# Odd query tiles' attention probabilities transposed by a trip through DRAM and VectorE instead of TensorE

## The reference

```
Q = x @ Wq;  K = ctx @ Wk;  V = ctx @ Wv            (8 heads)
score = Q K^T / sqrt(512), masked;  attn = softmax(score over the 77 keys)
out = concat_heads(attn @ V) @ Wo + x
y = (out - mean(out)) * rsqrt(var(out) + 1e-5) * gamma + beta
```

## Time and profile before

| | |
|---|---|
| time, three runs | 354.24 us median (353.8 to 354.63) |
| span of the profiled execution | 352.2 us |
| time around the span (median less span) | 2.0 us |
| PE busy | 346.3 us, 98% |
| DVE / ACT / POOL busy | 81% / 69% / 61% |
| TensorE's granted clock | full speed throughout |
| DMA | 55.81 MB, mean 158 GB/s |

### The profile page before, as it was taken

The page is one execution under the profiler, slowest core; times in us unless marked ns, Lnnn a source line. Parts: engine busy times, 40 slices in busy tenths (PEclk is TensorE's granted clock), DMA queues, the critical chain, the costliest instruction groups (busy, mean ns, idle before and its releaser), DMA issues.

```text
span 352.2 us, 6867 instructions
## 1 busy us (share of the span) xinstructions
PE 346.3 (98%) x2272; PEld 322.7 (92%) x2272; DVE 285.9 (81%) x523; ACT 243.3 (69%) x796; POOL 213.2 (61%) x218
## 2 busy tenths in 40 slices
PE   8999999999999999999999999999999999999994
PEld 6999999999999999998899899889988998999884
DVE  0159999999778767898798888987987989889896
ACT  3267766545777679887886976977778769768460
POOL 0045654400447958689769678688696696884243
PEclk9999999999999999999999999999999999999999
DMA  7998669775644080043152341440532413413012
GB/s 234 428 416 334 265 222 337 288 259 211 220 152 198 0 292 11 1 179 125 57 179 64 118 151 60 152 147 36 180 105 75 162 71 129 149 47 105 32 50 100
DMA packets 19683, 55.81 MB, mean 158 GB/s; under 512 B 1728, under 2 KB 3264, under 8 KB 17728
## 3 DMA queue, kind: packets, MB, share of 16 engines
q1 hardware_dynamic: 18784, 54.38, 42.8%
q10 hardware_dynamic: 864, 1.00, 1.0%
HBM read 46.98 MB, written 8.39 MB: 157 GB/s over the span
## 4 chain that ended last, share of the span: by engine, by line
PE 97%; DMA 1%; DVE 0%; DVEq 0%; issue 0%
PE pair L681 30%; PE pair L606 27%; PE pair L489 20%; PE pair L496 13%; PE pair L668 5%; PE pair L596 1%; PE pair L698 1%; DMA w_proj<-wk 1%; DVE centred L1199 0%; DVEq L105 0%; DVE stats_last L1191 0%; DVE mean_var L1196 0%; DVE var_eps L1171 0%; PE pair L616 0%; DVE out_sb L1185 0%
## 5 line engine op out<-in xcount | busy, mean ns | idle before, releaser
L1373 POOL TENSOR_TENSOR w_proj_lo<-w_proj,w_proj_hi 128x768 fp32r<-128x768 f32 x20 | 36.6, 1850 | 73.0 <-ACT w_proj_hi L766 73.0
L681 PE MATMUL pair<-vw_hi,pt_hi 128*128 128x512 f32 x155 | 62.3, 402 | 0.0
L681 PE MATMUL pair<-vw_hi,pt_lo 128*128 128x512 f32 x155 | 60.8, 392 | 0.0
L681 PE MATMUL pair<-vw_lo,pt_hi 128*128 128x512 f32 x155 | 60.6, 391 | 0.0
L1322 POOL TENSOR_TENSOR out_sb<-centred,beta_sb 128x512 f32<-128x512 f32 x30 | 38.9, 1296 | 28.9 <-ACT centred L875 28.8
L830 ACT ACTIVATE prob<-c,neg_max 128x77 f32<-128x77 f32 x128 | 44.0, 346 | 0.0
L489 PE MATMUL pair<-kv_t,w_out_hi 128*128 128x308 f32 x160 | 41.7, 334 | 0.0
L1367 POOL TENSOR_TENSOR xo_lo<-x_sum,xo_hi 128x512 fp32r<-128x512 f32 x32 | 41.4, 1299 | 0.2 <-ACT xo_hi L854 0.2
L606 PE MATMUL pair<-a_hi,xo_hi 128*128 128x308 f32 x128 | 40.4, 315 | 0.0
L606 PE MATMUL pair<-a_hi,xo_lo 128*128 128x308 f32 x128 | 38.9, 304 | 0.0
L606 PE MATMUL pair<-a_lo,xo_hi 128*128 128x308 f32 x128 | 38.9, 304 | 0.0
(11 more groups left out here) (117 smaller groups left out, 1015.1 us busy)
## 6 DMA issues: line engine op xcount, KB each, us to landing
w_out<-wo SPq DMA_DIRECT2D x8, 1024.0 KB, 4.8
xt_in<-x_tiles SPq DMA_DIRECT2D x16, 512.0 KB, 4.1
x_in<-x_rows SPq DMA_DIRECT2D x16, 512.0 KB, 4.9
out<-out_sb SPq DMA_DIRECT2D x31, 256.0 KB, 2.2
w_out<-wq_t SPq DMA_DIRECT2D x7, 1024.0 KB, 8.0
w_proj<-wv SPq DMA_DIRECT2D x8, 768.0 KB, 4.9
w_proj<-wk SPq DMA_DIRECT2D x6, 768.0 KB, 9.7
w_out<-wq_t SPq DMA_DIRECT2D x2, 512.0 KB, 8.0
```

What stands on the lines that cost most here:

```text
L681: mm = pe.matmul(ps_out[:, i % 2, 0:s.model], ps[:, j, :], v[:, j, b, :], start=(j == 0 and n == 0), stop=(j == s.key_t - 1 and n == len(p ...
L1373: pool.tensor_tensor(half_cols(w_proj_lo[u % W_RING], half), half_cols(w_proj_sb[u % W_RING], half), half_cols(w_proj_hi[u % 2], half).bit ...
```

## The change

Tiles 3, 5, ... 29 (fourteen, one in each iteration p = 2 to 15) no longer pass through PE's transposes. For them SP waits for the normalised probabilities, writes them to a DRAM tensor "shelf" in two DMAs (shelve), waits for these to land, and reads them back in four DMAs (take_back) into an SBUF tile "turned" in which the four 32-row groups of the queries and the four 32-key groups have changed places. DVE then turns 32x32 blocks in two instructions (turn) into ps_pt, after which ACT and DVE split as before. The even tiles, and tiles 1 and 31, stay on PE. DVE runs turn(a-1) where it ran split_pt(a-1), and split_pt(a-1) after normalise(a); ACT runs split_pt(a-1) after exps_first(p) instead of before it. The blocks need a key order with a stride: a group of 128 keys is now every third key of the first 384, or every second of the last 256 (key_tile), in prob and in VW alike, and both are padded from 616 to 640 keys with zeros. So VW's groups 0 to 2 are turned in uses 13, 14, 15 and groups 3 and 4 both in stage 2's first_products(0), where before they went in uses 10, 12, 13, 15 and one in first_products(0).

```diff
 def transposes_during(s):
-    plan, j = [], 0
-    for h in range(s.heads + 1):
-        ready = []
-        while j < s.key_t and j * P + s.key_rows(j) <= s.keys * h:
...
+    plan = [[] for _ in range(s.heads + 1)]
+    (_, first), _ = s.parts()
+    for j in range(first):
+        plan[s.heads - first + j] = [(j, b) for b in range(s.batches)]
+    plan[s.heads] = [(j, b) for b in range(s.batches) for j in range(first, s.key_t)]
...
+        turned = sb("turned", [P, P // QUAD, s.key_t * QUAD])
+        shelf = [nc.dram_tensor(f"shelf{n}", [P, P // QUAD, s.key_t * QUAD], F32, kind="Internal")
+                 for n in range(2)]
...
+        def key_tile(t, j):
+            first, count = s.parts()[j >= s.parts()[1][0]]
+            return t[:, first * P + j - first:(first + count) * P:count]
+        def by_dma(i):
+            return i % 2 == 1 and 3 <= i < LAST
...
+            def shelve(i):
+                n = dma_before(i)
+                sp.wait_ge(dve_prob, i + 1)
+                for first, count in s.parts():
+                    sp.dma_start(shelf[n % 2][:, :, first * QUAD:(first + count) * QUAD],
+                                 prob[i % 2][:, first * P:(first + count) * P].rearrange("p (c n) -> p c n", c=P // QUAD))\
+                      .then_inc(shelved[n % 2], DMA_INC)
+            def take_back(i):
+                n = dma_before(i)
+                sp.wait_ge(shelved[n % 2], 2 * use(n, 2))
+                if n > 0:
+                    sp.wait_ge(dve_turned, 2 * n)
+                by_quad = shelf[n % 2].rearrange("(r q) c n -> c q r n", q=QUAD)
+                for c in range(P // QUAD):
+                    sp.dma_start(turned[c * QUAD:(c + 1) * QUAD, :, :], by_quad[c]).then_inc(back, DMA_INC)
...
                 t = i - OUT_RING
+                if t >= 0 and by_dma(i):
+                    shelve(i)
+                    take_back(i)
...
                 for j in range(s.key_t):
-                    rows = s.key_rows(j)
-                    mm = pe.transpose(ps_pt[0:rows, j // 4, (j % 4) * P:(j % 4 + 1) * P],
-                                      prob[i % 2][:, j * P:j * P + rows], identity[:, :])
+                    mm = pe.transpose(ps_pt[:, j // 4, (j % 4) * P:(j % 4 + 1) * P],
+                                      key_tile(prob[i % 2][:, :], j), identity[:, :])
...
                 out_rows(a - 3)
-                transpose_prob(a - 1)
                 product_s3(p)
...
             def split_pt(i):
-                act.wait_ge(pe_pt, i + 1)
+                if by_dma(i):
+                    act.wait_ge(dve_turned, 2 * dma_before(i + 1))
+                else:
+                    act.wait_ge(pe_pt, pe_before(i + 1))
...
+                exps_first(p)
                 split_pt(a - 1)
-                exps_first(p)
                 scale(a - 3)
...
+            def turn(i):
+                dve.wait_ge(back, DMA_INC * (P // QUAD) * dma_before(i + 1))
+                dve.wait_ge(dve_pt_lo, i)
+                for first, count in s.parts():
+                    blocks = pt_blocks[:, first:first + count, :].rearrange("p j (r q) -> p r j q", q=QUAD)
+                    rows = turned[:, :, first * QUAD:(first + count) * QUAD].rearrange("p r (q j) -> p r j q", j=count)
+                    dve.transpose(blocks, rows).then_inc(dve_turned, 1)
...
-            split_vw(H, [0])
+            split_vw(plan[H][:1])
             add_w2(0)
             max_c11(0)
+            split_vw(plan[H][1:2])
             combine_c22(0)
             combine_c12(0)
             combine_c21(0)
-            split_vw(H, [1])
+            split_vw(plan[H][2:])
             normalise(0)
...
                 combine_c12(p)
-                split_pt(a - 1)
+                turn(a - 1)
                 combine_c21(p)
                 normalise(a)
+                split_pt(a - 1)
                 residual(a - 2)
```

More of the change, by code:

```diff
@@ L38 @@
 HALF_LOWEST = -3.0e38
-PAD_FROM = 96
+QUAD = 32
 class Shapes:
@@ L60, in __init__, with parts @@
         assert 2 * self.toks <= BANK and self.model <= BANK and self.dim_t == self.model_t == 4
-        assert self.batches == 2
-    def key_rows(self, j):
-        return min(P, self.row - j * P)
+        assert self.batches == 2 and self.key_t == 5
+    def parts(self):
+        return ((0, 3), (3, 2))
 def transposes_during(s):
-    plan, j = [], 0
-    for h in range(s.heads + 1):
-        ready = []
-        while j < s.key_t and j * P + s.key_rows(j) <= s.keys * h:
-            ready += [(j, b) for b in range(s.batches)]
-            j += 1
-        plan.append(ready)
+    plan = [[] for _ in range(s.heads + 1)]
+    (_, first), _ = s.parts()
+    for j in range(first):
+        plan[s.heads - first + j] = [(j, b) for b in range(s.batches)]
+    assert (s.heads - first) * s.keys >= first * P
+    plan[s.heads] = [(j, b) for b in range(s.batches) for j in range(first, s.key_t)]
     return plan
@@ L103, in build @@
     group_no = {g: n for n, g in enumerate(groups)}
+    early = sum(len(part) for part in plan[:H])
     with ExitStack() as stack:
@@ L181, in build @@
         c12 = sb("c12", [P, s.half])
-        sb("gap2", [P, 288])
-        prob1 = sb("prob1", [P, s.row])
+        prob1 = sb("prob1", [P, s.padded])
         neg_max = [sb(f"neg_max{n}", [P, H]) for n in range(2)]
@@ L200, in build @@
         u2, w2 = u2_w2[:, 0, :], u2_w2[:, 1, :]
-        prob = [sb("prob0", [P, s.row]), prob1]
+        prob = [sb("prob0", [P, s.padded]), prob1]
         assert s.dim_t * s.toks == s.row
-        kv_full = [prob1[:, :].rearrange("p (m k) -> p m k", m=s.dim_t),
+        kv_full = [prob1[:, 0:s.row].rearrange("p (m k) -> p m k", m=s.dim_t),
                    t_tmp4[0][:, :, :].rearrange("p a n -> p (a n)").rearrange("p (m k) -> p m k", m=s.dim_t)]
@@ L224, in build, with ps_vw @@
         ps_outp = pairs[2:4]
-        def ps_vw(h, b):
-            return (ps_proj[1] if h < H - 1 else ps_proj[0] if h < H else ps_outp[1])[:, b, :]
+        def ps_vw(j, b):
+            n = group_no[j, b]
+            return (ps_proj[1][:, b, :] if n < early - 2 else ps_proj[0][:, b, :] if n < early
+                    else ps_outp[b][:, (n - early) % 2, :])
         ld_ctx, ld_mask, ld_gamma, ld_beta = sem("ld_ctx"), sem("ld_mask"), sem("ld_gamma"), sem("ld_beta")
@@ L263, in build @@
         dve_centred, dve_pad, dve_last = sem("dve_centred"), sem("dve_pad"), sem("dve_last")
+        shelved = [sem(f"shelved{n}") for n in range(2)]
+        back, dve_turned = sem("back"), sem("dve_turned")
         pool_const, pool_p_lo = sem("pool_const"), sem("pool_p_lo")
@@ L295, in head_cols, with dma_before, pe_before @@
             return t[:, 2 * half:2 * half + 2, :, h * s.keys:(h + 1) * s.keys]
+        def key_tile(t, j):
[3 more added lines that the diff above has]
+            return i % 2 == 1 and 3 <= i < LAST
+        def dma_before(i):
+            return sum(by_dma(t) for t in range(i))
+        def pe_before(i):
+            return i - dma_before(i)
         def tile_cols(w, m):
@@ L595, in transpose_vw @@
                     for m in range(s.model_t):
-                        mm = pe.transpose(ps_vw(h, b)[0:rows, m * P:(m + 1) * P],
-                                          vw_t[:, m, b, j * P:j * P + rows], identity[:, :])
+                        mm = pe.transpose(ps_vw(j, b)[:, m * P:(m + 1) * P], key_tile(vw_t[:, m, b, :], j),
+                                          identity[:, :])
                     mm.then_inc(pe_vw, 1)
@@ L674, in out_rows @@
                 pe.wait_ge(dve_pt_lo, i + 1)
-                if i >= 2:
+                if i < 2:
+                    pe.wait_ge(dve_vw_lo, early + 3 + i)
+                else:
                     pe.wait_ge(dve_centred, i - 1)
@@ L793, in split_vw @@
                 for j, b in plan[h]:
-                    rows = s.key_rows(j)
                     act.wait_ge(pe_vw, group_no[j, b] + 1)
[L796 to L799, removed]
+                    act.activation(vw_hi[:, j, b, :], ps_vw(j, b)[:, 0:s.model], ACT.Copy).then_inc(act_vw_hi, 1)
             def seed(p):
@@ L1030, in add_out_product, with split_vw, clear_pads @@
                 dve.tensor_tensor(cols, by_batch(second(ps_outp[half])), cols, ALU.add).then_inc(dve_vw_sum, 1)
[L1032 to L1036, removed]
-                    dve.wait_ge(act_vw_hi, group_no[j, b] + 1)
[L1038 to L1046, removed]
+            def split_vw(parts):
+                for j, b in parts:
+                    dve.wait_ge(act_vw_hi, group_no[j, b] + 1)
+                    dve.tensor_tensor(vw_lo[:, j, b, :], ps_vw(j, b)[:, 0:s.model],
+                                      vw_hi[:, j, b, :].bitcast(F32), ALU.subtract).then_inc(dve_vw_lo, 1)
+            def clear_pads():
+                dve.wait_ge(act_t_hi, len(T_PARTS))
+                dve.wait_ge(dve_t_lo, len(T_PARTS))
+                dve.wait_ge(pe_outp, 2 * (USES - 1))
+                for n in range(2):
```

(7 more changed lines are left out.)

26 lines of the change are left out of this document (12 added, 14 removed).

## The result

The changed kernel takes **372.89 us** (median of 4 runs, 372.4 to 375.33) against 354.33 us before (median of 4, 353.8 to 354.63): ratio 1.054, 95% interval 1.051 to 1.057. That is 18.6 us slower, where +4.7 was forecast; the direction was right, the size was outside the range (347 to 371). The profiled execution's span is 371.2 us, 19.0 more than before's.

The account below looks back on a forecast made before the run. The prediction took PE, 98% busy, as the present bound and a loop of 8.1 + 6.1 = 14.2 us as the new one: 13 x 0.31 = 4.0 us plus 0.7 gives +4.7, about 359 us; range 347 to 371.

Parts of the forecast that it names:

- A new loop: Stage 2: normalise, DRAM trip, turn and VectorE's in-order work set a period of 14.2 us against 13.89; chance 0.48.
- PE's saving: Stage 2: dropping an odd tile's five transposes saves PE 0.54 us per iteration, 7.6 us over fourteen if nothing else binds.
- R: Round trip through DRAM from the end of normalise(a-1) until turn(a-1) can start: 6.1 us, lowest 5.1, highest near 10.
- The loop's fixed part: VectorE's work in the loop besides the round trip, from turn to the end of the next odd normalise: 8.1 us.
- the turn itself: VectorE's two block transposes per odd tile, 384 and 256 elements: 0.54 and 0.41 us, 0.8 us with overlaps.
- the way out: Writing 320 KB of probabilities to DRAM: 1.2 us fixed plus 1.6 us for 1,024 pieces, 2.8 us.
- The last return: Last of four read-back DMAs, 80 KB: fixed part 1.5 us plus 0.3, landing 1.8 us after its issue.
- The start and the strided transposes: VW's moved transposes at tile 0 and PE's strided even-tile transposes: zero, with +0.5 us at most at the start.
- The end: PE's transposes of tile 30 wait for split_pt(29), 3.7 us after turn(29) starts instead of 3.0: 0.7 us more.
- Small writes at double cost: Rival: trip-out pieces cost twice 25 ns, the write takes 3.2 us, R is 7.7, time about 380 us; chance 0.08.
- Block transposes at half rate: Rival: VectorE's turn takes 1.6 us instead of 0.8, loop 15.0 us, time near 370 us; chance 0.05.
- Hidden trip: Rival: the DRAM trip is short, R 5.1 us, PE's full 7.6 us come off, 346.6 us; chance 0.33.

Follow-up runs that it names:

- run 4: Changed kernel with one more 2 KB DMA, which nobody waits for, issued by SP in front of each trip's writes: 380.57 us, ratio 1.075.
- run 5: Changed kernel with the trip's two writes in pieces made one write of whole 2,560-byte rows, keys then in wrong order: 360.9 us, ratio 1.020.
- run 1: Changed kernel without the trip through DRAM; VectorE turns a constant tile instead, odd tiles 3 to 29 not computed: 351.26 us, ratio 0.992.
- run 2: Changed key order, padding and later VW transposes alone; all tiles turn on TensorE in the old order: 356.66 us, ratio 1.007.
- run 3: Changed kernel without the DRAM trip, plus one extra VectorE transpose of 640 elements before each turn, result unread: 355.93 us, ratio 1.004.
- run 6: Changed kernel with SP waiting for the return to land before issuing the next store and loads of x: 375.17 us.
- run 8: Changed kernel with turn(a-1) moved behind combine_c21 and normalise(a) on VectorE, and ScalarE's split behind scale: 365.99 us, ratio 1.035.
- run 9: Changed kernel with the turn late, ScalarE's split of tile a-1 behind exps_second(p), VectorE's behind moments(a-2): 376.7 us, ratio 1.063.
- run 10: Changed kernel with the turn late and ScalarE's split of tile a-1 between four and four heads of exps_second(p): 360.07 us, ratio 1.015.

## Why the prediction was right and wrong

- **A new loop decides, not PE's saving: right.** The waits stood where they were forecast, in front of all turns but the first; the period is 8.24 + R in every iteration. Runs 4 and 5 are the same loop at two other values of R (7.34 and 5.99 in the mean), and without the trip (run 1) the waits are gone.
- **The loop's fixed part, 8.1 us: right,** measured 8.24. The difference is the turn itself, 0.95 us from start to start instead of 0.8: the instruction of 384 elements took 0.70 us where 0.54 had been put down, the one of 256 took 0.43 for 0.41.
- **R = 6.1 us: this term failed.** It is 6.83 in the mean. In a quiet trip (the one at 251.44) the way out took 3.07 us (251.44 to 254.51) where 2.8 had been put down. The packets were as assumed (1.47 us for 1.6); but the sum had put nothing for the issue between the two writes, and the second goes out 0.60 us behind the first. The three gaps of the return took 1.33 for the 1.4 put down. The last return took 2.14 us for 1.8: its fixed part is longer than the assumed 1.5. That makes 6.54. The rest up to 6.83 is mostly four long trips of 7.2 to 7.6 us, and no scatter had been put in. 0.73 us x 13 = 9.5 of the 13.9 us that were missed.
- **Why the time lies outside the range.** R = 6.83 alone would not have done it: by the prediction's own sum it gives 13 x (8.1 + 6.83 - 13.89) + 0.7 = 14.2 us, or about 368.5, and the range allowed R up to 7.0. What took it over 371 are the next three items together. The range covered R and left every other term at its value.
- **The turn's 0.15 us** more than assumed: 13 x 0.15 = 2.0 us.
- **The start and the strided transposes: put at zero, 0.9 us in this kernel** before turn(3), 2.4 in run 2. In the changed kernel the stride's 0.04 us a tile is hidden behind the loop.
- **The end: 0.7 put down, 2.5 measured.** PE's wait in front of tile 30 was foreseen and made 1.0. That it would come back from 3.7 us of idleness at half the clock, and take 1.6 us more for a tile's transposes and out_rows, was not.
- **Small writes at double cost (rival, 0.08): no.** Pieces of 384 bytes took 24 ns each and of 256 bytes 16 ns by the trace's packets, 1.47 us in all against 0.98 for the whole rows of run 5 (104 ns for each 2,560 bytes). The Trainium skill (DMA: Bandwidth & Descriptors, Specifications) has transfers under 512 bytes as read, change and write; if so, these runs show it at no more than 1.5 times, and R at 6.8, not 7.7. They show no boundary at that size: the return's pieces of 640 bytes took 40 ns each, the same 16 bytes per ns.
- **Block transposes at half rate (rival, 0.05): no;** 640 elements took 0.83 us in run 3, as any other pass.
- **Hidden trip (rival, 0.33): no.** Had it been hidden, the gain would have been 3.0 us (run 1), not 7.6: 2.4 us go to the key order, and PE's period in run 1 is 13.54, 0.15 above what its removed instructions leave after the stride, which are the two longer steps behind its wait for VectorE.

Open: what makes some trips long (run 6), and whether a trip given a whole pair more, out_rows(a-1) one iteration later, would reach run 1's 351.3 us. Runs 8 to 10 move the turn by 2 us only; a pair's delay changes the order of all tiles behind softmax and was not tried.

## What to carry to other kernels

Where an in-order engine waits for a round trip that its own earlier instruction started, write down the loop: its work from the wait to the next start of a trip, plus the trip. If that is above the bound engine's period, the trip paces everything, and every fixed part of it (issues in series, two landings) counts in full in each iteration; give its length a range as wide as its fixed parts are uncertain, and multiply that by the iterations. To move the wait down the list helps only until the next engine's list closes a loop through the same instruction: follow ScalarE's and TensorE's orders before moving it.

## What the runs showed of the hardware

- SP needs 0.60 us to issue a write of 512 pieces (1.21 for two), 0.34 for one of 128 whole rows, 0.44 for a return of 128 pieces of 640 bytes, and 0.26 for one row of 2 KB.
- The trip to DRAM and back with two waits, 320 KB: 6.45 us at best, 5.51 at best with whole rows on the way out.
- TensorE, after 3.7 us without work, was granted 0.54 of its clock over the next 3 us. In run 10 a wait of 2.56 us and in run 3 one of 1.98 us were followed by 3.4 us at 0.50; in run 8's profiled execution a wait of the same 2.56 us was not.
- VectorE's 32x32 block transpose of 640 fp32 elements from SBUF to SBUF took 0.83 us, as an ordinary pass; the one of 384 elements into PSUM took 0.70.
- PE's transposes of every third or second 4-byte column: 0.50 us for five instead of 0.47.
